# One transformer layer on one core: the prologue, the block period and the router re-ordered, with filling matmuls before the first expert

## The reference

```
h = weight[x]                                    # x: 8 x 1024 tokens, width 256
n = layernorm(h)
qkv = n @ qkv_proj.T + qkv_bias                  # q, k, v: 256 wide, 16 heads of 16
attn = softmax(q . k / 4)                        # 8 x 8 for each column and head
h = h + (attn @ v) @ out_proj.T + out_bias
n = layernorm(h)
scores = sigmoid(n @ Wg.T)                       # 16 experts in 4 groups
choice = scores + bias_corr
# a group's score is the sum of its two best; the 2 best groups stay; of them the 4 best experts
w = scores at the 4, divided by their sum, times 2.5
h = h + sum_e w_e * (relu(n @ W1[e].T)**2 @ W2[e].T) + relu(n @ Ws1.T)**2 @ Ws2.T
```

## Time and profile before

| what | value |
|---|---|
| median of 3 runs | 1339.79 us (1339.21 to 1339.84) |
| the profiled execution's own time | 1341.05 us |
| its span, first to last instruction | 1339.3 us |
| mean granted TensorE clock | 0.977 |
| PE busy | 1228.9 us, 92% |
| weight loads (PEld) busy | 1020.1 us, 76% |
| DVE busy | 1067.7 us, 80% |
| ACT busy | 630.1 us, 47% |
| POOL busy | 524.8 us, 39% |
| ACT table loads | 33 of 1283 ns |

### The profile page before, as it was taken

The page is one execution under the profiler, slowest core; times in us unless marked ns, Lnnn a source line. Parts: engine busy times, 40 slices in busy tenths (PEclk is TensorE's granted clock), DMA queues, the critical chain, the costliest instruction groups (busy, mean ns, idle before and its releaser), DMA issues.

```text
span 1339.3 us, 19873 instructions
## 1 busy us (share of the span) xinstructions
PE 1228.9 (92%) x7488; PEld 1020.1 (76%) x7488; DVE 1067.7 (80%) x1726; ACT 630.1 (47%) x1072; POOL 524.8 (39%) x723
## 2 busy tenths in 40 slices
PE   1755999999999999999999999999999999999998
PEld 0342887878787887878788787878878788887887
DVE  1667979798897979889797988889797888979653
ACT  2144354545545454554545454454545445454443
POOL 6261535336063533516253451625344161514100
PEclk9867999999999999999999999999999999999999
DMA  3021112212121222212122221212122122212121
GB/s 116 0 83 60 63 48 80 80 65 79 49 80 47 81 79 65 79 49 80 49 95 63 73 71 49 80 59 85 64 80 64 60 72 73 67 48 80 64 95 64
DMA packets 34128, 91.66 MB, mean 68 GB/s; under 512 B 4720, under 2 KB 13296, under 8 KB 34032
## 3 DMA queue, kind: packets, MB, share of 16 engines
q1 hardware_dynamic: 30960, 81.99, 18.2%
q0 software_dynamic: 3072, 8.39, 2.5%
HBM read 81.46 MB, written 8.91 MB: 67 GB/s over the span
## 4 chain that ended last, share of the span: by engine, by line
DVE 45%; PE 28%; ACT 10%; issue 10%; POOL 4%; DVEq 2%; DMA 1%; ACTq 0%; POOLq 0%; SPq 0%
DVE hid_lo L663 10%; PE psB L932 8%; DVE ring L692 7%; PE psY L905 7%; PE psH L890 6%; DVE r_sb L658 6%; DVE ring L300 4%; PE psA L973 4%; DVEq L741 2%; DVE ring L320 2%; ACT p_sb L522 2%; DVE o_sb L327 2%; DVE stats L675 2%; ACT hid_hi L524 2%; ACT L598 1%
## 5 line engine op out<-in xcount | busy, mean ns | idle before, releaser
L905 PE MATMUL psY<-w_hi,hid_hi 128*128 128x256 f32 x1152 | 327.4, 284 | 21.4 <-DVE h L669 21.4
L522 ACT ACTIVATE p_sb<-r_sb 128x512 f32<-128x512 f32 x288 | 180.9, 628 | 346.8 <-DVE r_sb L658 345.7
L905 PE MATMUL psY<-w_lo,hid_hi 128*128 128x256 f32 x1152 | 323.5, 281 | 0.0
L905 PE MATMUL psY<-w_hi,hid_lo 128*128 128x256 f32 x1152 | 323.2, 281 | 0.0
L905 PEld LDWEIGHTS psY<-w_hi,hid_hi 128*128 128x128 f32 x1152 | 216.8, 188 | 50.2 <-issue 39.2
L663 DVE TENSOR_TENSOR hid_lo<-p_sb,hid_hi 128x512 fp32r<-128x512 f32 x288 | 232.7, 812 | 27.2 <-ACT hid_hi L524 26.8
L890 PE MATMUL psH<-xT_hi,w_hi 128*128 128x512 f32 x576 | 233.8, 406 | 0.0
L890 PE MATMUL psH<-xT_lo,w_hi 128*128 128x512 f32 x576 | 228.3, 396 | 0.0
L890 PE MATMUL psH<-xT_hi,w_lo 128*128 128x512 f32 x576 | 228.2, 396 | 0.0
L905 PEld LDWEIGHTS psY<-w_lo,hid_hi 128*128 128x128 f32 x1152 | 216.8, 188 | 11.0
L320 POOL TENSOR_TENSOR ring<-ring 128x512 f32<-128x512 f32 x96 | 126.6, 1318 | 239.6 <-DVE ring L692 239.6
(11 more groups left out here) (132 smaller groups left out, 1977.8 us busy)
## 6 DMA issues: line engine op xcount, KB each, us to landing
cwB<-cw_dram SPq DMA_DIRECT2D x128, 512.0 KB, 3.8
out<-h SPq DMA_DIRECT2D x32, 256.0 KB, 3.2
h<-w_t SPq DMA_DIRECT2D x3, 512.0 KB, 3.9
xin<-table,idx POOLq DMA_INDIRECT x64, 3.8
p_sb<-w_t SPq DMA_DIRECT2D x4, 256.0 KB, 4.2
cwB<-w_t SPq DMA_DIRECT2D x4, 256.0 KB, 3.4
ring<-wqkv_t SPq DMA_DIRECT2D x2, 384.0 KB, 3.3
cwB<-w_t SPq DMA_DIRECT2D x1, 512.0 KB, 3.8
```

Source lines behind the costliest of these rows:

```text
L522: nc.scalar.activation(p_sb[:, n % 2, :], r_sb[:, n % 2, :], ACT.Square)
L905: last = nc.tensor.matmul(psY[:, j // 2, (j % 2) * D:(j % 2 + 1) * D], hid[a][:, e % R, j * P:(j + 1) * P], W2[b][:, e, :], start=(e == 0 ...
```

## The change

Six things are changed.

1. The tables of places and the loops over them are gone. Every engine has a prologue written out call by call, and a function `period(b)` with its calls in a new order. The cut between prologue and periods is the same as before: prologue up to `spread_probs` 0 and 1 of block 1.
2. Each of the 14 weight pieces has a place of its own (`home`), so no load waits for a place. The loads of the shared and routed experts' pieces are issued after the first gather has landed. The two constants for output bias and router bias have a semaphore of their own (`wide_in`) and are loaded after the first eight pieces.
3. POOL's constants are made in three parts; each is waited for where it is used (`CONST_IDENT`, `CONST_SMALL`, `CONST_ALL`). The gather of block 1 is issued after all of them.
4. `product` and `score` take the heads' halves one after the other (`lp, ih = t % LP, t // LP`), not alternately: products 0 to 3 need only the first q and the first k piece.
5. The choice of experts is 22 single groups (`route(blk, 0)` to `route(blk, 21)`), each waiting at its head for the one before it, so other calls can stand between any two. A drain is gone. One table set is loaded ahead of all ACT work by name.
6. PE has 17 calls `warm(4)` in the prologue: each issues 4 matmuls of 512 columns to `psY` on the first weight piece; nothing reads their result. In block 0 DVE sums slots 1, 3, 5 and 7, afterwards 3 and 7 as before.

The core of the diff:

```diff
-        stage = [rows(cwB[:, 0, :, :]), rows(cwB[:, 1, :, :]), rows(p_sb[:, :, :]), rows(h1[1][:, :, :])] + \
-                [rows(ring[:, k, :, :]) for k in range(4)]
+        home = [rows(q_sb[:, :, :]), rows(v_sb[:, :, :]), rows(o_sb[:, :, :]), rows(o_sb[:, :, :])[:, T:],
+                rows(ring[:, 0, :, :]), rows(ring[:, 0, :, :])[:, T:],
+                rows(ring[:, 1, :, :]), rows(ring[:, 2, :, :]), rows(ring[:, 3, :, :]),
+                rows(h1[0][:, :, :]), rows(p_sb[:, :, :]), rows(cwB[:, 0, :, :]), rows(cwB[:, 1, :, :]),
+                rows(h1[1][:, :, :])]
...
-        SUMS_VECTOR = (3, 7)
+        SUMS_VECTOR = ((1, 3, 5, 7), (3, 7))
...
-            lp, ih = t // KH, t % KH
+            lp, ih = t % LP, t // LP
             if lp == 0:
                 eng.wait_ge(qkv_ready, nth(blk, 6, 2 * (ih + 1)))
+            if blk == 0 and t == 0:
+                eng.wait_ge(w_lo, RING_FREE)
...
+            sp.wait_ge(xin_in[0], 16 * TT)
+            for k in range(PIECES_ATT, PIECES_SHARED + 2):
+                piece_in(k)
+            sp.dma_start(bo_sb[:, :], bo.partition_broadcast(P)).then_inc(wide_in, 16)
+            sp.dma_start(bc_sb[:, :], bias_corr.partition_broadcast(P)).then_inc(wide_in, 16)
+            for k in range(PIECES_SHARED + 2, PIECES_ALL):
                 piece_in(k)
...
+            def period(b):
+                if b + 1 < B:
+                    sum_of(b + 1, 2)
+                if b + 2 < B:
+                    rstd_of(0, b + 2)
+                if b + 1 < B:
+                    sum_of(b + 1, 4)
+                    sum_of(b + 1, 5)
+                    sum_of(b + 1, 6)
+                    rstd_of(1, b + 1)
+                if b + 3 < B:
+                    gather(b + 3)
+                if b + 1 < B:
+                    root_of_sum(b + 1)
+                if b + 2 < B:
+                    sum_of(b + 2, 0)
+                    sum_of(b + 2, 1)
+                    bias_in(b + 2)
...
+            nc.scalar.preload_act_table_set("natural_log_exp_and_others")
...
+                if g > 0:
+                    dve.wait_ge(route_step, nth(blk, ROUTE_STEPS, g))
...
+            def warm(count):
+
+                pe.wait_ge(w_hi, 1)
+                for k in range(count):
+                    nc.tensor.matmul(psY[:, k % 2, :], WQKV[0][:, 0, 0, :],
+                                     WQKV[0][:, 0, 0:4, :].rearrange("p c i -> p (c i)"), start=True, stop=True)
```

More of the change, by code:

```diff
@@ L505, in _ @@
+            root_of_sum(0)
+            sum_of(1, 0)
+            sum_of(1, 1)
+            bias_in(1)
+            for b in range(B + 1):
+                period(b)
         @block.scalar
@@ L639, in _ @@
+            transposed_hi(1, 0)
+            exponent(1)
+            router(0)
+            probs_high(1)
+            square(0, 0)
+            qkv_out(1, 5)
+            weights_out(0)
+            weight_hi(13)
+            square(0, 1)
+            for b in range(B + 1):
+                period(b)
         @block.vector
@@ new lines, in probs_low @@
+            def probs_low(blk):
+                dve.wait_ge(probs_hi, nth(blk, 1, 1))
+                for ih in range(KH):
+                    rows = slice(64 * ih, 64 * ih + 64)
+                    last = nc.vector.tensor_tensor(pr[ih][64 - 64 * ih:128 - 64 * ih, :],
+                                                   s_sb[rows, :, :].rearrange("p m n -> p (m n)"),
+                                                   pr[ih][rows, :].bitcast(f32), ALU.subtract)
+                last.then_inc(probs_lo, 1)
@@ new lines, in _ @@
+            weight_lo(0)
+            weight_lo(1)
+            norm_stats(0, 0)
+            weight_lo(2)
+            weight_lo(3)
+            transposed_lo(0, 0)
+            weight_lo(4)
+            weight_lo(5)
+            weight_lo(6)
+            weight_lo(7)
+            weight_lo(8)
+            product(0, 0)
+            product(0, 1)
+            product(0, 2)
+            product(0, 3)
+            product(0, 4)
+            product(0, 5)
+            product(0, 6)
+            product(0, 7)
@@ new lines, in _ @@
+            weight_lo(9)
+            scores_max(0)
+            weight_lo(10)
+            scores_sum(0)
+            weight_lo(11)
+            probs_low(0)
+            norm_stats(0, 1)
+            weighted_values(0, 0)
+            weighted_values(0, 1)
+            sum_of(0, 1)
+            weighted_values(0, 2)
+            weighted_values(0, 3)
+            weighted_values(0, 4)
+            weighted_values(0, 5)
+            sum_of(0, 3)
+            weighted_values(0, 6)
+            sum_of(0, 5)
@@ new lines, in _ @@
+            transposed_lo(0, 1)
+            weighted_values(0, 7)
+            sum_of(0, 7)
+            attention_lo(0, 0)
+            product(1, 0)
+            attention_lo(0, 1)
+            product(1, 1)
+            product(1, 2)
+            product(1, 3)
+            residual(0)
+            product(1, 4)
+            product(1, 5)
+            weight_lo(12)
+            product(1, 6)
+            product(1, 7)
+            transposed_lo(1, 0)
+            scores_max(1)
+            route(0, 0)
@@ L876, in _ @@
+            route(0, 20)
+            route(0, 21)
+            probs_low(1)
+            hidden_lo(0, 0)
+            weighted_values(1, 0)
+            weight_lo(13)
+            weighted_values(1, 1)
+            for b in range(B + 1):
+                period(b)
         @block.tensor
@@ new lines, in _ @@
+            out_projection(0)
+            qkv(1, 3)
+            qkv(1, 4)
+            score(1, 0)
+            score(1, 1)
+            score(1, 2)
+            score(1, 3)
+            score(1, 4)
+            score(1, 5)
+            transpose_rows(1, 0)
+            score(1, 6)
+            score(1, 7)
+            logits(0)
+            warm(4)
+            up(0, 0)
+            qkv(1, 5)
+            warm(4)
+            up(0, 1)
+            up(0, 2)
+            warm(4)
+            weights_transpose(0)
@@ L1053 @@
+            spread_probs(1, 0)
+            spread_probs(1, 1)
+            for b in range(B + 1):
+                period(b)
 def kernel(x, L0_tok_weight, L0_attn_qkv_proj, L0_attn_qkv_bias, L0_attn_out_proj, L0_attn_out_bias,
```

991 lines of the change are left out of this document (610 added, 381 removed).

## The result

The changed kernel takes 1297.4 us (median of 4 runs, 1296.51 to 1297.99), the kernel before beside it 1339.67 (1339.21 to 1339.84): ratio 0.9684, 95% interval 0.9668 to 0.9701. That is 42.3 us saved where 47.5 were forecast. The profiled execution took 1296.51 us, 1.8 above its span; before that was 1341.05.

A forecast was written before the change was run, and what follows sets the result against it. PE was taken as the bound: waiting in the prologue, then periods of about 74.5 us work and 2.9 lost. Prologue 27, periods 18 and tail 2.5 make 47.5 off 1339.8: 1292 us, range 1268 to 1318.

The forecast's parts named there:

- PE's new list has the same 74.5 us of work: In each period: PE's reordered calls were claimed to need unchanged work of about 74.5 us.
- The sum of the period: Steady period: 1.9 us lost for 2.9 now, 76.05 for 77.45 us, 1.4 less times 13 periods: 18 us.
- the rival of a failing prologue: Prologue: half clock stays or weight pieces come late, path keeps half its lead; 1317 us, chance 0.12.
- The turn: Between blocks: 3.8 us of cover before D0 removes PE's 1.7 us loss, with a margin of 0.6 to 1.7.
- The late softmax: In each period: probs_low ends after PE is due at spread 0, costing 1.2 us for the old 0.4.
- full-gain rival: No late softmax in the periods and a prologue lead of 31: 71 us saved, 1269 us, chance 0.2.
- The table loads: Each router: two 1.28 us loads go, gain inside the softmax's 1.2; if they stay, score 0 waits 2 us.
- The prologue: Start up to block 1's first spread: leads add to 30.7 us, of which 27 were taken; bounds 15 and 33.
- no semaphore step between the seven milestones: Prologue: reason given for taking 27 of the 30.7 us lead, as such steps had not been priced.
- The second rival: Only the prologue gains: POOL's bias_in behind the turn's sums eats its margin, 1.4 us lost again; 1310 us, chance 0.15.
- The slower rival: Softmax's fixed order in one DVE queue delays score 0; decides from 2.3 us a period above 77.45; chance 0.05.
- The tail: Last two periods: 2.5 us of the last but one's 4.9 lost come back, last nothing; bounds 0 and 4.5.

The follow-up runs named there:

- Experiment 1: Kernel before with only products and scores taking one half of the heads after the other: 1390.48 us, ratio 1.0376 to the kernel before.
- experiment 2: Changed kernel with alternating halves from block 2 on, product 1 moved later and scores split two and two: 1263.62 us, ratio 0.9429 to the kernel before.
- experiment 5: Changed kernel with down(b, 0) ahead of spread 3 and up 4, a shorter cover at the turn: 1311.58 us, ratio 0.9775 to the kernel before.
- experiment 4: Changed kernel without the table set loaded by name: 1314.5 us, ratio 0.9804 to the kernel before.
- experiment 6: Changed kernel without SP's wait for the first gather, all weight loads issued at once: 1301.96 us, ratio 0.9707 to the kernel before.
- experiment 3: Changed kernel without any filling matmuls: 1298.29 us; run again side by side, 1298.91 us without and 1296.28 us with them.
- experiment 10: Changed kernel with POOL's bias_in ahead of root_of_sum, beside the products again: 1317.31 us, ratio 0.9822 to the kernel before.
- experiment 7: Changed kernel with router groups 0 to 20 in one row on DVE in each period: 1349.81 us, ratio 1.0062 to the kernel before.

## Why the prediction was right, and where not

The forecast of 1292 us lies 5.4 us under the measured 1297.4, and the range of 1268 to 1318 holds it. But that is in part luck, for it is a sum of errors of both signs: the prologue gave 5.6 us more than forecast, the tail 3.0 more, and the 13 periods 11.5 less.

**The step that failed** is "PE's new list has the same 74.5 us of work". The list has the same calls, and the same 32 score matmuls of the same duration, but 3.1 us more of work, because of the order of the halves, which puts neighbouring scores onto the same rows of `psB`. Experiment 1 shows it with that line alone (+3.4 us a period, +51 us in all), experiment 2 takes it back (74.66 us a period). The Trainium skill, "TensorE: Matmul & The Clock Gate", section "Part 3: Packing small matmuls — row/col tiling" (and its list "Why this matters for your kernels"), has matmuls with small outputs run at the same time if their outputs start at different strips of 32 partitions. The runs agree: four instructions start within 0.02 us where they write four strips, two where they write two, and the next group 0.43 us later in both.

**The sum of the period** was also added up wrongly. The terms of the prediction are 74.5 of work and 1.2 + 0.4 + 0.3 = 1.9 of loss, that is 76.4, not 76.05; the 0.5 that the projection "keeps" isn't in it at all. By its own terms the period gains 1.05 us and the 13 periods 13.7, not 18, and the time would have been 1296.6, nearer to the measured one for no good reason: the measured gain of 6.5 us is made of other things. In the same way the rival of a failing prologue takes 10 us off for the rest where its own sum has 18 + 2.5, and no reason is given.

**The turn** was right: D0 waits for nothing, the 1.7 us of the earlier trace rows are gone, and the margin is 0.8 us (experiment 5).

**The late softmax** was a term of 1.2 us that did not come. With the slower scores DVE waits 2.27 us ahead of `scores_max` and PE for nothing at all. In experiment 2, where the scores are quick, the wait exists, at 0.5 us: the term was mis-sized by more than twice, and the 0.7 for weighted values and small ones was not seen. So a period of 74.7 was there to be had, where the forecast had 76.05 and the full-gain rival 74.5. That rival's 1269 us was the right price of a kernel with this order and the old halves; experiment 2 runs at 1263.6.

**The table loads** were said to be no term of their own and 2 us of wait for score 0 if they stay. With the loads back (experiment 4) a period is 1.0 us longer and the kernel 16: hidden in another term was a gain of 13 us in the 13 periods, of the 18 that were forecast for all of them. What was read rightly is the price of one. The trace of experiment 4 has the load 0.01 us behind the activation before it (541.24 + 0.26) and the next activation 0.01 us behind the load, 0.02 in the earlier trace rows; the Trainium skill, "ScalarE: Activation LUTs", section "What ACT_TABLE_LOAD costs", adds a drain of 1.38 us, which these rows don't show.

**The prologue** gave 32.6 us for 27. The gather came 2.8 us earlier (experiment 6 puts the whole effect of the later loads at 4.4 at the first stats). The transposed input was complete at 21.78, 4.6 us earlier than before, where only the gather's 2.0 were counted; the fills in front of q/k/v cost 0.8, close to the 1.0 of the prediction, so q/k/v started at 22.59 for 25.4, the products began at 26.50 for 30, the spread of block 1 came at 99.05 for 102, "103 to 106". The lead at that spread is 33.6 us, and 32.6 are left at the first add_experts; so of the 3.7 us taken off since "no semaphore step between the seven milestones" was priced, only 1.0 was lost. The clock, said to be at 1.00 from about 30 us, was not: it is 0.86 in the mean of 45 to 70 us and 0.94 from 70 to 100. The fills bring the clock but hardly time (experiment 3): the path there is DVE's.

**The second rival**, that bias_in at the turn eats the margin, named the right mechanism and the wrong place. At the turn it costs PE nothing. Beside the products, in the new order of POOL, it costs 1.5 us a period with the clock's part (experiment 10). That is the worth of its place in this order, and not a gain over the kernel before, where it lengthened a product by only 0.3 us. The Trainium skill, "SBUF — State Buffer", section "Who interferes with whom", says that two inputs in SBUF are enough for VectorE to contend with GpSimd's reads. It agrees with the product of 3.16 us, and the end 1.09 us after POOL's, nearly the 1.22 of a product alone, looks like waiting until POOL's instruction has ended and not like a slower pace. At the turn it agrees too, the other way round: hid_lo, with two inputs in SBUF, had begun 0.05 us earlier, keeps its 0.68, and POOL's instruction takes 2.89 for 2.40. Which place is the dear one, the rule doesn't say; the rows do.

**The slower rival** was a real way to lose: with the router in one row (experiment 7) the router's groups delay the products and these the scores, the 13 periods are 80.3 us in the mean, above the 79.8 from which the rival was said to decide, and the kernel is 0.6% slower than before. In the profiled executions 43.2 us are lost in 13 periods, 4.9 before the first add_experts (187.6 for 182.7) and 5.3 in the last but one. Without the clock's part the periods are 79.6, just short of that limit. The order of the change is not near that point.

**The tail** gave 5.5 for 2.5, above its bound of 4.5: all that PE lost in the last but one period and the clock's 0.97 came back (59.59 busy of 59.60 us at 1.00).

Open: what the fills are worth below 2.6 us, why the clock in experiments 7 and 10 falls in some periods only though the pause is in all, and whether the strips or the shared weights let neighbouring scores start together.

## What to carry to other kernels

When a change renumbers which slice of an output an instruction writes, count its cost anew: the same matmuls with the same durations cost nearly twice as much (7.12 us for 3.98) once their neighbours no longer write other strips. The count and the mean duration hide that; the group's busy time and the distance between starts show it. And when an engine has no pause left but the period didn't shrink, its work grew: compare start-to-start sums by call, before looking for waits.

## What the runs showed of the hardware

- Matmuls with 32 output rows and 512 columns start in groups 0.43 us apart: four in a group where neighbours write four different strips (0.12 us each), two where they write two (0.22 us each); each lasts 0.59 to 0.62 us either way.
- A VectorE product of two SBUF inputs, 1.22 us alone, takes 3.16 us when it meets a GpSimd tensor_tensor of 2.4 us: it ends 1.09 us after GpSimd's end, in all 13 meetings of experiment 10. Where the VectorE instruction began first (0.05 us, at the turn), it kept its 0.68 us and GpSimd's took 2.89.
- With the later weight loads issued ahead of the first gather's landing, its rows are used at 14.87 us, for 10.18 to 11.20 in the eleven profiled executions that hold them back.
- A table load of ScalarE takes 1.28 us, with 0.01 us from the activation before it and 0.01 to the one behind (experiment 4).
- A pause of PE of 0.7 us and sixteen small matmuls were followed by a fall to 1.2 GHz (mean clock 0.62 over 4.5 us) in five of twelve periods, 1.5 us each (experiment 10); a pause of 2.05 us by one within the eight matmuls behind it (0.53 over 3.5 us) in seven of twelve, 1.3 to 1.8 us each (experiment 7). In the other periods the same pause left the clock at 1.00.
